# Causal heads: TensorE does the steps between heads in the middle of the next batch, and their readers follow one chunk later

## The reference

```python
x = L0_attn_x                                               # (2, 1024, 128)
x = _layernorm(x + _L0_attn_ref(x, ...), axis=-1)           # causal, 16 heads of 8
x = _layernorm(x + _L0_ffn_ref(x, ...), axis=-1)            # router, top 2 of 8 experts, relu
x = _layernorm(x + _L1_attn_ref(x, ...), axis=-1)           # causal, q and k of low rank (q_a q_b)
x = _layernorm(x + _L1_ffn_ref(x, ...), axis=-1)            # attention without a mask, then experts, gelu
...
attn = scale * jnp.einsum('bhqd,bhkd->bhqk', q, k)
attn = jnp.where(causal[None, None], attn, -jnp.inf)
attn = jax.nn.softmax(attn, axis=-1)
ans = jnp.einsum('bhqk,bhkd->bhqd', attn, v)
```

## Time and profile before

| | |
|---|---|
| median of 3 runs | 1224.54 us (1223.82 to 1226.81) |
| profiled execution | 1223.02 us, of which the span is 1221.2 us |
| TensorE busy | 1105.6 us (91% of the span) |
| VectorE busy | 864.5 us (71%) |
| ScalarE busy | 777.3 us (64%) |
| GpSimd busy | 281.8 us (23%) |
| mean granted TensorE clock | 0.986 of full speed |
| first causal attention | about 34 to 305 us of the span |
| second causal attention | about 446 to 708 us |

### The profile page before, as it was taken

The page is one execution under the profiler, slowest core; times in us unless marked ns, Lnnn a source line. Parts: engine busy times, 40 slices in busy tenths (PEclk is TensorE's granted clock), DMA queues, the critical chain, the costliest instruction groups (busy, mean ns, idle before and its releaser), DMA issues. The chain is left out here.

```text
span 1221.2 us, 24980 instructions
## 1 busy us (share of the span) xinstructions
PE 1105.6 (91%) x8797; PEld 605.1 (50%) x8872; DVE 864.5 (71%) x2072; ACT 777.3 (64%) x1569; POOL 281.8 (23%) x824
## 2 busy tenths in 40 slices
PE   5899998999999989999988999788888988899996
PEld 3466676655776755666655642222112221137774
DVE  3788767784334467888776889899999989904433
ACT  4366656667444426677666658878888878874443
POOL 8134322333102113433332431111101010100001
PEclk9799999999999999999999999999999989999998
DMA  3444343110000801243312221101111100000000
GB/s 88 118 115 109 96 96 87 49 31 12 1 1 1 184 10 32 59 105 94 85 49 65 55 43 36 24 16 24 36 36 36 23 11 16 7 1 1 10 9 18
DMA packets 40058, 57.71 MB, mean 47 GB/s; under 512 B 9494, under 2 KB 15078, under 8 KB 39678
## 3 DMA queue, kind: packets, MB, share of 16 engines
q1 hardware_dynamic: 39934, 56.11, 18.8%
HBM read 30.81 MB, written 24.64 MB: 45 GB/s over the span
## 5 line engine op out<-in xcount | busy, mean ns | idle before, releaser
L851 ACT ACTIVATE probs<-bank 128x512 f32<-128x512 f32 x1088 | 574.9, 601 | 240.8 <-PE bank L1210 239.8
L950 DVE TENSOR_REDUCE tile_max<-bank 128x1 f32<-128x512 f32 (+3 forms) x1152 | 611.9, 592 | 40.2 <-PE bank L1195 35.6
L1195 PE MATMUL bank<-qk 125*128 125x128 bf16 (+2 forms) x1664 | 389.1, 312 | 66.8 <-DVE tile_max L950 47.0
L1210 PE MATMUL bank<-qk 128*128 128x128 bf16 (+4 forms) x1608 | 362.6, 305 | 5.7 <-ACT probs L851 5.3
L1239 PE MATMUL bank<-probs,v_head 128*32 128x512 f32 (+3 forms) x3328 | 302.9, 453 | 0.1
L1195 PEld LDWEIGHTS bank<-qk 125*128 125x128 bf16 (+1 forms) x1664 | 132.4, 97 | 313.7 <-DVE tile_max L950 243.0
L1117 DVE SCALAR_TENSOR_TENSOR acc<-bank,gate,acc 128x128 f32<-128x128 f32 x256 | 71.9, 343 | 156.7 <-PE bank L1372 156.7
L1239 PEld LDWEIGHTS bank<-probs,v_head 128*32 128x32 f32 x3328 | 139.6, 109 | 52.7 <-issue 29.8
L1210 PEld LDWEIGHTS bank<-qk 128*128 128x128 bf16 (+1 forms) x1664 | 133.1, 97 | 57.2 <-ACT probs L851 21.0
L871 ACT ACTIVATE probs<-bank,sb_b 128x512 f32<-128x512 f32 x128 | 81.0, 684 | 117.9 <-PE bank L1361 117.9
L944 DVE TENSOR_REDUCE tile_max<-bank 128x4 f32<-128x512 f32 x128 | 87.4, 687 | 90.0 <-PE bank L1195 89.9
(11 more groups left out here) (132 smaller groups left out, 664.2 us busy)
## 6 DMA issues: line engine op xcount, KB each, us to landing
qk<-qk_parts SPq DMA_DIRECT2D x160, 144.0 KB
qk_parts<-q_parts SPq DMA_DIRECT2D x48, 192.0 KB, 2.4
qk_parts<-k_parts SPq DMA_DIRECT2D x48, 192.0 KB, 3.2
qk_parts<-q_parts SPq DMA_DIRECT2D x24, 96.0 KB, 2.3
qk_parts<-k_parts SPq DMA_DIRECT2D x24, 96.0 KB, 2.9
sb_w<-in_w SPq DMA_DIRECT2D x8, 256.0 KB, 3.6
sb_w<-in_w SPq DMA_DIRECT2D x2, 1024.0 KB, 5.2
qk<-neg_rows SPq DMA_DIRECT2D x96, 6.0 KB
```

The lines of the kernel that those rows point to most:

```text
L851: nc.scalar.activation(probs[:, hd.probs_place(c), :], S2[i % len(S2)][:], ACT.Exp, scale=hd.a.scale).then_inc(sem("probs"), 1)
L950: ins = nc.vector.tensor_reduce(tile_max[:, hd.slot, t, which:which + 1], s1[:, at:at + P * count], AX.X, ALU.max)
L1195: ins = mm(s1[:, at:at + P * count], qk[hd.query_rows, hd.place, 0, P * t:P * (t + 1)], qk[hd.query_rows, hd.place, 1, P * k0:P * (k0 + co ...
L1210: ins = mm(s2[:, at:at + P * count], qk[hd.key_rows, hd.place, 1, P * j:P * (j + 1)], qk[hd.key_rows, hd.place, 0, P * q0:P * (q0 + count) ...
```

## The change

In the causal heads TensorE now does the steps of a place not at the end of its batch but in the next batch after that batch's second chunk; ScalarE and VectorE read after the third chunk, and VectorE's `rests` after the fourth. Causal heads are so treated as the others are.

```diff
         if self.a.causal:
             self.place = g % RING
-            self.read_after = 1
...
         else:
-            self.read_after = 2
...
-                        if c == batch[hd.read_after] and before is not None:
+                        if c == batch[2] and before is not None:
                             between(before)
...
-                        if c == batch[hd.read_after] and before is not None:
+                        if c == batch[2] and before is not None:
                             between(before)
-                        if c == batch[hd.read_after + 1] and before is not None:
+                        if c == batch[3] and before is not None:
                             rests(before)
...
-                        if c == batch[1] and before is not None and not HEADS[before[1]].a.causal:
+                        if c == batch[1] and before is not None:
                             between(before)
...
-                    if hd.a.causal:
-                        between(at_head(g, k))
```

## The result

The changed kernel takes 1220.37 us (median of 6 runs, 1218.96 to 1220.62) against 1224.42 us in the same comparison (6 runs, 1223.76 to 1226.81): a ratio of 0.9964, interval 0.9952 to 0.9976. That is 0.36% faster. It lies inside the stated range, but beyond the 0.3% up to which the likeliest case went, so in the part to which I had given a chance of 0.2. The profiled execution (1220.30 us) has a span of 1218.4 us, 2.8 less than the one before (1221.2).

A forecast was written before the change was run, and what follows sets the result against it. Causal heads were taken as bound by TensorE's own work, 15.0 us a pair. The terms, -4.9 + 7.3 - 3.0 + 1.0 - 0.7 = -0.3 us, took the median 1224.54 to 1224.2 us; range 1218.5 to 1229.5.

The forecast's parts named there:

- the likeliest case: Whole kernel: waits only change places, time within 0.3% of before, 1221 to 1228 us; chance 0.6.
- the rival "faster": Steps in causal heads are well covered: sum -9.4 us, with two thirds of it -6 us, 1218.5; chance 0.2.
- waits for `neg_rows`: TensorE's steps in causal heads no longer wait for ScalarE's `rows`: gain 4.9 us, bounds 3.5 and 5.7.
- waits at the bank's next tenant: `turn_sums` and `max_rows` wait longer for readers of the shared bank: +7.3 us, bounds 4 and 12.
- waits for row maxima: In stretches with steps, VectorE catches up during mid-batch steps; half the waits go: gain 3.0 us, bounds 0 and 5.9.
- entering and leaving a step: Mid-batch in causal heads, 0.09 us charged to 12 steps using part of the array: +1.0 us, bounds 0 and 6.3.
- the clock: TensorE's low clock at 634 to 636 us: half of up to 1.4 us won back, gain 0.7, bounds 0 and 1.4.
- The rival that took its price from the other heads: Each of 35 mid-batch steps costs 0.18 us, as in heads without a mask: sum +5.0, 1229.5 us; chance 0.2.

The follow-up runs named there:

- ScalarE early: From the changed kernel: ScalarE of causal heads reads after the second chunk, VectorE's `rests` after the third, its other steps unchanged; 1208.73 us, ratio 0.9885.
- `root` first: GpSimd does `root` in causal heads before the quarters and second mask: on the changed kernel 1218.63 us, on that with ScalarE early 1208.51 us.

## Why the prediction held, and what it had wrong

The sum was -0.3 us with the rival "faster" at a chance of 0.2; measured is -4.1 by the medians (-2.8 by the profiled spans). The range held because it was wide; the sum itself missed, since four of its five terms came out lower than predicted, by 0.5 to 1.4 each. The mechanism was right: what went and what came are the waits that I named, and the experiments that undo one half each show both. Term by term, from the waits of the two traces:

| term | predicted | in the profile |
|---|---|---|
| waits for `neg_rows` | -4.9 | -5.6 (5.9 to 0.3) |
| waits at the bank's next tenant | +7.3 | +6.8 (6.0 to 12.8) |
| waits for row maxima | -3.0 | -4.2 (10.0 to 5.8) |
| entering and leaving a step | +1.0 | about -0.4 |
| the clock | -0.7 | 0 |

*Waits for `neg_rows`.* Of the 2.0 us 0.3 is left, not 0.8. That these waits and those at `max_rows` are in series I did not see; it does little harm here, since both sizes came out near.

*The bank's next tenant.* The turn-round read from rows 5 to 7 gave 0.7, 1.55, 0.4 and 1.25 for a copy and a `qk` at `turn_sums` and at `max_rows`; the trace shows 0.6, 1.3 to 1.5, 0.4 and 1.1 to 1.2. The kernel with TensorE alone moved shows that it is the readers' lateness: 2.6 us in place of 12.8. For the eight `eff` I took nothing, and they cost 1.0, of which 0.4 is in the +6.8.

*Row maxima.* "I take half" was too careful: 4.2 of 10.0 us go; of the 5.9 that I had in view 4.3 go. The kernel with ScalarE early, against that with TensorE alone moved, puts 4.5 us of these waits on VectorE's own late steps.

*Entering and leaving* is the step that failed. I charged part of what a step costs in mid-batch of the other heads, and bounded the term by zero from below. In fact `proj` is 0.11 us cheaper in mid-batch than at the end of a batch, `aT` and `xT` 0.05, `v` and the first two `qk` 0.1, and `logits` with its 16 products 0.3 (2.02 from its start to the next scores before, 1.70 now). Their first weight load runs under the scores; that this is the reason fits the rows above, and no run tried it alone. Dearer are steps that use a part of the array: `eff` (64 rows) and `gb` (8 rows) by some 0.1 each, and `qk` of layer 2 (64 columns) by 0.09. `gateT`, a transpose onto 8 columns, to which I had charged 0.09 too, follows the scores after 0.22 and costs nothing more. The Trainium skill, "TensorEngine Tiling (Array Packing)", section Key Properties, says that a change of tiling mode drains TensorE; the trace agrees in that the 0.09 of entering appears for `eff`, `gb` and `qk` of layer 2 and not for `proj`. For `gateT` it does not appear, and why not is open. The rival that took its price from the other heads is out by the 0.22 and 0.89 of `proj` alone. That the load does not run ahead of its product at the end of a batch can be read in the same way (the products with v are on 32 columns), but no run here moved that alone.

*The clock.* The stretch of low clock is still there, 3.4 us long as before, though the 1.2 us wait is down to 0.2, so the part that I counted on did not come. With `root` first it goes, and others come in the heads without a mask. Nor does the 2.0 us wait bring it each time: in the kernel with TensorE alone moved the same wait of 2.0 ends at 624.5 us, and the clock stays at its higher level behind it. So it does behind the wait of 3.26 with step and reader after the first chunk. The two rows, in this order, with the columns of the earlier trace rows:

```profile
624.00:640.00 16.00, 14.34 (x145) 9.41 (x149) 9.88 (x21) 13.46 (x30) 4.54 (x15) 1.00 0.32 102
625.00:640.00 15.00, 14.77 (x147) 9.57 (x150) 9.60 (x20) 12.47 (x28) 3.33 (x11) 1.00 0.31 103
```

The terms sum to -3.4 in the traces, where the starts of `max_rows` say -3.1 over both attentions. That they agree so well is in part luck: small groups that the table leaves out, waits for `probs` and idle time put down to `issue`, rise together by 1.3 from 60 to 712 us, and waits too short to be listed fall. The profiled spans differ by 2.8 and the medians by 4.1; most of the last 1.2 us lies in the profiled execution of the kernel before, which took 1223.02 us where the median is 1224.42.

One sum of the prediction is wrong in itself: its own lower bounds of the five terms (-5.7, +4, -5.9, 0, -1.4) add up to -9.0, not to -14.4. The range does not rest on it, but the rival "faster" at -9.4 so stood beyond the bounds, and should have been called an extreme.

## What to carry to other kernels

When a producer's step is moved, its readers need not follow by as much: ask for each reader when its input is there, what stands ahead of it in its own queue, and who waits for it to be done. Here the best place of ScalarE's reading was behind the last exp whose scores were made before the step. One place later it is late by the step's own length, and with a buffer that has one tenant at a time the next tenant pays for it (bank waits of 12.8 us against 2.6). One place earlier, with the step, it is in the way of the exps (waits for `probs` of 6.9 us against 1.6). Ask it for each engine by itself: here ScalarE's readings and the `rests` early and VectorE's other steps late gives 1.15% where the change as it stood gave 0.36%.

## What the runs showed of the hardware that was not expected

- An fp32 step between bf16 scores on the whole array costs 0.05 to 0.11 us less than behind products on 32 columns (`logits` 0.3 less), with its first weight load running ahead (207.39 against the product's 207.60).
- Idle time of TensorE and low clock do not go together one to one. Behind the wait of 2.0 us for GpSimd near 630 us the clock is at 1.2 GHz for 3.4 us in the kernel before, in the change, in the one with only the readers moved and in the one with the step after the first chunk. Behind the same 2.0 us with TensorE alone moved, behind 1.84 us with ScalarE early, and behind 3.26 us of idle time at 625 us with step and reader after the first chunk it stays at 2.4 GHz. What sets off such a stretch, the runs don't show.
- Time won in one stretch was given back in another, where the granted clock was low for longer. With `root` first, 2.9 and 1.9 us were won near 625 us. From the last causal head through the heads without a mask, where the edit changes nothing, TensorE was at 1.2 GHz for 13.7 us in both, where the kernels without this edit had 6.8 and 10.2, and 2.7 and 1.7 us went there. One execution of each kernel is traced, and the mean granted clock of the nine of the kernel before in that group goes from 0.981 to 0.987, so that the edit causes it is not shown; the medians of the untraced runs, though, don't show the gain either.
